# Local attention layers: first two tiles' scores and first maximum ahead of the last tiles' transposes and inverse norm

## What is computed

```python
for l in range(DEPTH):                    # DEPTH = 2
    h = shift_token(x)
    q, k, v = split(h @ wqkv[l], 3)       # 8 heads of 64
    q, k = l2norm(q) * qs, l2norm(k) * ksc
    q, k = rotary_xpos(q, k)
    sim = 8 * q @ k.T                     # windows of 64 queries, 128 keys, causal band mask
    x = x + softmax(sim) @ v @ wo
    h = layernorm(shift_token(x)) * lg + lb
    a, g = split(h @ w1 + b1, 2)
    x = x + (a * gelu(g)) @ w2 + b2
```

## Time and profile before

| | value |
|---|---|
| median of three runs | 2535.45 us |
| profiled execution, device time | 2529.74 us |
| its span, first to last instruction | 2527.8 us |
| PE / DVE / ACT / POOL busy | 83% / 76% / 57% / 24% of the span |
| mean granted TensorE clock | 0.924 of 2.4 GHz |
| chain that ended last, by engine | PE 43%, DVE 37%, ACT 13%, issue 5% |

### The profile page before, as it was taken

The page is one execution under the profiler, slowest core; times in us unless marked ns, Lnnn a source line. Parts: engine busy times, 40 slices in busy tenths (PEclk is TensorE's granted clock), DMA queues, the critical chain, the costliest instruction groups (busy, mean ns, idle before and its releaser), DMA issues.

```text
span 2527.8 us, 48854 instructions
## 1 busy us (share of the span) xinstructions
PE 2105.7 (83%) x18320; PEld 1242.4 (49%) x18320; DVE 1932.4 (76%) x4231; ACT 1431.2 (57%) x2618; POOL 603.2 (24%) x480
## 2 busy tenths in 40 slices
PE   5996889787799588877889958887788995898877
PEld 3674233556467333364647723336464762334645
DVE  7756998787755799778685579976778458997776
ACT  4343677747334277674733437767463343786755
POOL 2622001331253100225034210030505330004040
PEclk9997899898899799989989969998998996999989
DMA  4002100110000210101000030010100002001010
GB/s 152 1 1 75 30 8 15 25 25 14 18 1 1 76 32 6 22 19 32 13 9 1 1 89 19 9 32 7 32 13 9 1 15 75 19 11 33 5 32 21
DMA packets 63892, 63.25 MB, mean 25 GB/s; under 512 B 22000, under 2 KB 49200, under 8 KB 63152
## 3 DMA queue, kind: packets, MB, share of 16 engines
q1 hardware_dynamic: 60472, 57.27, 9.1%
q10 hardware_dynamic: 3192, 2.90, 0.4%
HBM read 24.68 MB, written 15.01 MB: 16 GB/s over the span
## 4 chain that ended last, share of the span: by engine, by line
PE 43%; DVE 37%; ACT 13%; issue 5%; DMA 1%; SPq 0%; DVEq 0%; ACTq 0%
PE PS L1381 40%; DVE arena L1135 17%; ACT arena L749 7%; DVE arena L1235 2%; PE PS L1692 2%; DVE s_at L1210 1%; DVE arena L1203 1%; DMA tmp<-xf 1%; ACT arena L696 1%; PE PS L1399 1%; DVE tmp L1210 1%; DVE arena L1322 1%; ACT tmp L703 1%; ACT x_in L763 1%; DVE xn L888 1%
## 5 line engine op out<-in xcount | busy, mean ns | idle before, releaser
L1381 PE MATMUL PS<-arena 128*32 128x256 f32 (+5 forms) x11328 | 803.5, 328 | 165.8 <-DVE arena L1135 77.3
L1381 PEld LDWEIGHTS PS<-arena 128*32 128x32 f32 (+5 forms) x11328 | 373.6, 120 | 595.2 <-DVE arena L1135 294.5
L1135 DVE TENSOR_REDUCE arena<-PS 128x1 f32<-128x512 f32 x1024 | 639.2, 683 | 19.7 <-PE PS L1381 19.1
L696 ACT ACTIVATE arena<-PS 128x1024 f32<-128x1024 f32 x512 | 519.4, 1028 | 196.7 <-PE PS L1381 196.0
L651 ACT ACTIVATE arena<-PS 128x512 f32<-128x512 f32 x256 | 150.8, 598 | 245.1 <-PE PS L1381 244.9
L1381 PEld LDWEIGHTS PS<-w2e,arena 128*128 128x128 f32 x2048 | 246.0, 192 | 50.1 <-issue 49.8
L1097 DVE TENSOR_TENSOR arena<-PS,arena 128x512 f32<-128x512 f32 x128 | 86.4, 689 | 214.5 <-PE PS L1381 214.1
L1381 PE MATMUL PS<-w2e,arena 128*128 128x128 f32 x2048 | 247.5, 275 | 0.1
L749 ACT ACTIVATE arena<-PS,arena 128x128 f32<-128x128 f32 x512 | 230.8, 545 | 20.2 <-DVE arena L1272 18.9
L502 POOL TENSOR_TENSOR zz<-zz,arena 128x512 f32<-128x512 f32 x104 | 135.4, 1302 | 271.1 <-DVE arena L1097 242.5
L1381 PE MATMUL PS<-wqkv,arena 128*128 128x512 f32 x384 | 176.7, 598 | 21.7 <-ACT arena L731 21.7
(11 more groups left out here) (306 smaller groups left out, 3271.5 us busy)
## 6 DMA issues: line engine op xcount, KB each, us to landing
arena<-arena SPq DMA_DIRECT2D x120, 128.0 KB, 2.3
scr_q<-arena SPq DMA_DIRECT2D x40, 128.0 KB, 2.4
scr_k<-arena SPq DMA_DIRECT2D x40, 128.0 KB, 2.4
arena<-scr_k SPq DMA_DIRECT2D x24, 200.0 KB
arena<-scr_q SPq DMA_DIRECT2D x24, 192.0 KB
scr_m<-arena SPq DMA_DIRECT2D x256, 1.0 KB
x_in<-in_x SPq DMA_DIRECT2D x5, 512.0 KB, 4.7
arena<-scr_m SPq DMA_DIRECT2D x128, 2.0 KB
```

What stands on the lines that cost most here:

```text
L696: act.activation(pb[:, n % 8], pair(2 * (n % 2)), ACT.Exp).then_inc(S["p"], 1)
L1135: dve.tensor_reduce(mxp[:, blk % 2, j, t, hf:hf + 1], PS[:, ring_bank(m), :], AX, ALU.max)\
L1381: return pe.matmul(o, w, v, start=start, stop=stop, **kw)
```

## The change

`EARLY` becomes 2, and a new constant `LATE` = 3 says how many `keep` calls ACT leaves for its second phase. No instruction is added or removed; the streams around the seam become:

- PE: ... `qkv(7)`, `kq(3)`, `scores(0)`, `kq(4)`, `scores(1)`, `kq(5)`, `scores(2)`, `kq(6)`, `scores(3)`, transposes of tile 0, `kq(7)`, `scores(4)`, ...
- ACT: ... square root, table load, `keep(4)`, exponentials 0, `keep(5)`, exponentials 1, `keep(6)`, exponentials 2, copy, `keep(7)`, exponentials 3, ...
- DVE: ... squares' sum of tile 7, maximum 0, `inverse(6)`, maximum 1, normalisation 0, maximum 2, ...

```diff
-EARLY = 1
+EARLY = 2
+LATE = 3
...
-                    for t in range(T + LAG + 1 - EARLY):
+                    for t in range(T + LAG + 1 - LATE):
                         u = l * T + t
                         if t >= LAG + 1:
                             keep(t - LAG - 1)
...
-                            if 1 <= u <= EARLY:
-                                keep(T - EARLY + u - 1)
+                            if 1 <= u <= LATE:
+                                keep(T - LATE + u - 1)
                             act.wait_ge(S["ml"], n + 1)
...
+                    def top(u):
+
+                        n = T * l + u
+                        sv = PS[:, 2 * (n % 2):2 * (n % 2) + 2, :].rearrange("p r (c k) -> p r c k", k=KEYS)
+                        dve.wait_ge(S["s_lps"], n + 1)
+                        if n >= 2:
+                            dve.wait_ge(S["p_exp"], 8 * (n - 1))
+                        link(dve.tensor_reduce(ml[:, n % 2], sv, AX, ALU.max))
+
+                        dve.scalar_tensor_tensor(ml[:, n % 2], ml[:, n % 2], -1.0,
+                                                 rq[:, u, 0:HL].rearrange("p (c r) -> p r c", r=2),
+                                                 ALU.mult, ALU.mult).then_inc(S["ml"], 1)
+
+                    top(0)
                     inverse(T - 2)
...
-                        if u < T:
...
+                        if 1 <= u < T:
+                            top(u)
...
-                    for t in range(T + LAG):
+                    for t in range(T):
...
-                        if t < T:
-                            qkv(t)
+                        qkv(t)
...
                         if t >= LAG:
-                            if t - LAG >= T - EARLY:
-                                scores(t - LAG - (T - EARLY))
                             kq(t - LAG)
+                    for t in range(EARLY):
+                        scores(t)
+                        kq(T - LAG + t)
                     for u in range(T + 4):
                         n = T * l + u
                         if EARLY <= u + 1 < T:
                             scores(u + 1)
+                        if u == 1:
+                            kq(T - 2)
...
                                 ins.then_inc(S["pt_ps"], 1)
+                        if u == 2:
+                            kq(T - 1)
                         if 4 <= u <= T + 3:
```

## The result

The changed kernel takes 2489.72 us (median of 4 runs, 2489.26 to 2490.05); the kernel before took 2535.44 (median of 4, 2531.20 to 2536.01). The profiled executions, on which the sum was made, differ by less: 2490.05 (span 2488.1) against 2529.74 (span 2527.8), 39.7 us.

What follows compares the result with a forecast made beforehand. No single engine bounds the kernel, but ACT does after the seam. Holes of 33.1 us less 3.6 leave 29.5, say 30 us, off 2535.45: 2505.5 us, range 2498 to 2518.

Steps and rivals of the forecast that it cites:

- the meeting with POOL that I allowed for: DVE's product of maximum and norm may wait beside POOL's scaling: ml at 468.5, cost nothing; uncovered, 0.6 us a layer.
- the holes: ACT's idle time before exponentials (20.2 us) and between copies at the seam, together 33.1 us to be gained.
- ACT's stream without holes: Adding up ACT's exponentials and copies after keep(4): tile 3's exponentials start at 483.6, not 487.69, 4.1 us earlier.
- a late `kq(7)` at the lower clock: PE's last transposes delay tile 3's exponentials by 0 to 0.7 us, taken as 0.35 us a layer off the gain.
- handoffs: Handoffs that the holes had hidden take 0.1 us a layer off the gain.
- The rule that I cited from the Trainium skill: Multiplications with waits between them run cold; by it alone PE's lower clock lasts through the seam, giving 2516 us.
- The rival, 2516 us: PE's clock stays low through kq(7), scores(4) and the product with v: gain only 19.5 us; chance 12%.

Runs made afterwards that it cites:

- e3: Changed kernel with ACT waiting for the end of its own last exponential behind each of a layer's 8 tiles; 2501.68 us.
- e6: e3 with eleven more waits a layer, ACT waiting for the end of its own last copy; 2510.45 us.
- e11: Kernel before with both PE idle times around kq(4) filled by extra, uncounted scores(0) and scores(1); 2522.22 us.
- e5: Changed kernel with PE's two early scores each one step later, behind kq(4) and kq(5); 2504.17 us.
- e8: e5 with scores(0) also made once, uncounted, at its early place ahead of kq(4); 2492.15 us.
- e4: Changed kernel with ACT's keep(4) moved ahead of the square root of tiles 6 and 7; 2490.60 us.
- e7: e4 with three unread multiplications on PE in layer 1, between qkv(1) and qkv(2); 2489.85 us.

## Why the prediction was wrong

**What held.** That ACT is what ends last from `keep(4)` on, that its holes are what the change is worth, and that the gain passes on almost whole: the exponentials of tile 3 start 4.93 us earlier in the first layer (483.65 - 467.54 = 16.11 us after the table load, against 487.69 - 466.65 = 21.04), and its stage ends 4.83 us earlier. Putting the scores into PE's idle time cost nothing; the meeting with POOL that I allowed for came (the product took 0.85 us, `ml` at 469.27) and was hidden as I said: the first exponential came at 469.88, 0.47 us after the last copy of `keep(4)` started, that is, without a hole.

**The term that failed: the holes.** I took their price as the idle time that the profile shows, 33.1 us. In the trace it is 33.6 (the fourth small hole of the layers 0 was left out). From start to start they were worth 40.7: the exponentials of tile 3 came 21.04 to 21.27 us after the table load before, and 16.11 to 16.12 after. The 7.1 us between are the overlap that each wait for another engine takes away. The kernel before had 52 such holes, seven in each layer 0 (the four copies, the first exponential, the copy of tile 0's half, the exponentials of tile 3) and six in each layer 1, where tile 3 did not wait. Forty-four of them stretched the distance to the instruction ahead by 0.11 to 0.13 us more than the idle time shown (one by 0.16), and the eight copies of tile 0's half, behind an exponential and the reading of its sum, by 0.22 to 0.28, with no idle time in brackets at all (486.06 to 486.78 in the first layer, 0.72 us where exponentials follow each other every 0.44). That is some 7 us. Behind tile 3 the stages gave 0.65 us back, which leaves the 40.05. The breaks of e3 and e6 show the same price, 0.12 to 0.20 us for a break with next to no idle time. I had it before me in the other way of counting: ACT's stream without holes gave 4.1 us, which used 3.63 us for eight exponentials and 1.05 for two copies, durations with their latency in them. From start to start they take 3.49 and 0.94, and tile 3 comes at 16.1 and not 17.0 us after the load.

**The term that did not come.** I took off 0.35 us a layer for a late `kq(7)` at the lower clock and 0.1 for handoffs, 3.6 in all. The clock was low from some time after 472 to about 479 and up again before `kq(7)`, which took 1.04 us (480.76); no hole was left over in any of the eight layers. So 33.6 us of idle time and some 7 us of overlap, less the 0.65 us at the end of the stages, make up the 40.05.

**The clock.** In the sum I had it as a risk of the new order only; as a gain it stood just in the range, with 3 us. The runs showed the gain: the two scores fill the idle times behind which it fell before, and that is 1.4 us a layer in the old order (e11), and 1.1 to 1.9 if taken away from the new (e5, e8). The sum needed no term for this, since I priced the holes as they were, slow transposes included. The rule that I cited from the Trainium skill, "TensorE: Matmul & The Clock Gate", section "Loop structure matters more than you think", speaks of a long wait for a DMA between every multiplication, which is more than the shorter waits here. The trace agrees with my reading of it for 472 to 479, where PE worked in pieces between waits and ran at 0.53 of full speed, and disagrees for 462 to 472, where it also did and ran at 1.00. The slow stretch cost nothing, as ACT was full. The rival, 2516 us, did not come.

**The baseline.** The last 5.7 us of the 45.7 have no cause in the change. I set the sum against the median of three runs, 2535.45, and the kernel before gave 2531.2 to 2533.5 in all later ones. Against those the gain is 41 to 44 us. The stages' 40 us taken off the profiled execution's 2529.7 give 2489.7.

**The range.** Its lower end, 2498, was 37 us below the median of before, the holes and 3 us for the clock. It held no term for a price of a hole that the idle time doesn't show, so a gain of 40 us lay outside it even before the 5.7 us of the baseline.

**Open.** What decides at a given idle time of PE whether the clock drops, with the same work around it; what the 0.65 us behind tile 3 are; and what lies between span and device time, which was 1.8 to 2.2 us in the other profiled executions and 5.5 in e11's (2521.19 against 2515.7; 4.6 to 6.2 in all eight of its runs).

## What to carry to other kernels

Price a hole in the stream of the engine that is the bound from start to start of the instructions on either side of it, against the same pair without a wait; the idle time of the profile leaves out the overlap, here 0.11 to 0.28 us a hole. Where the granted clock falls behind an idle time of PE, here of 2.2 to 2.6 us, put there work that is due anyway, as this change does with its scores, before looking at what that work gives by itself. For single stages, measure from marks in the trace: here the changed kernel's eight stages agreed within 0.04 us, where whole runs of the kernel before scattered by 7. And when waits are added to price one, count the waits that the edit really makes, and which of them stand where the engine waits anyway.

## What the runs showed of the hardware

- Back-to-back ACT instructions overlap: copies that last 0.56 and 0.57 us start 0.46 to 0.47 us apart. A wait for the end of the instruction just ahead moved the next one's start by 0.12 to 0.20 us (e3, e6), of which 0.03 to 0.04 us stand in the trace as idle time.
- The same 2.19 us of idle PE was followed by a drop of the granted clock in all four passes of one kernel (e4), 1.7 us lost each time, and in none of another (the changed kernel). With three spare multiplications there (e7) it dropped in no pass.
- A DVE product of 8 elements a partition, from two SBUF operands, took 0.85 to 1.04 us beside POOL's L534 and 0.17 alone.
